# Decoder layer, attention: the turned row maxima, from a two-byte block to an f32 block

## The chip, the cores and the metric

One core of a Trainium2 chip runs the kernel. The metric is the device time of one execution in microseconds; the kernel before took 1079.38 us in the median of three runs (1075.42 to 1080.08).

## The reference

A decoder layer on x of shape (4, 512, 512) f32: attention, a quantised cross part and a feed-forward layer with routed tokens, each added to x behind a layer norm. Only attention matters here:

```
result, ch_bias, n = _chunk_decompose(hidden_states.reshape(bsz * tgt, H))
Q = (proj(q_weight, WQ, q_bias) * scaling).reshape(bsz, tgt, HEADS, HEAD_DIM)
K = proj(k_weight, WK, k_bias).reshape(bsz, tgt, HEADS, HEAD_DIM)
attn = jnp.einsum('bqhd,bkhd->bhqk', Q, K)
probs = jax.nn.softmax(attn, axis=-1)
ctx = jnp.einsum('bhqk,bkhd->bqhd', probs, V).reshape(bsz * tgt, H)
```

There are 32 heads of 16 channels, and the softmax subtracts the maximum over the keys of each row.

## The kernel before, in words

Attention runs in 32 iterations i, one for each batch and group of four heads (512 queries by 512 keys for each head). The first four and the last four are unrolled, 24 lie in a loop whose body holds four (`steps`, L351). Q and K of a group are kept as f16 parts, high and low, in rings of four buffers (QP, KP): rows 0 to 47 for two heads, rows 64 to 111 for the other two, so that two matmuls run beside each other in two halves of the array's rows.

Scores are computed twice. The first time (`scores`, L1284) queries lie on partitions: a pair of 128x512 blocks goes to two PSUM banks, and VectorE takes the negated maximum of each row (`maxima`, L854) into NM, a block of 128 queries by 16 (two halves `a` by eight steps `x`) for each iteration. This runs ahead: during iteration i, the pairs 1 to 7 are those of i+2 and pair 0 is the last one of i+1. The second time (L1332) keys lie on partitions, and two further rows of QP (rows 48, 49 and 112, 113, MROW) carry the maximum of each query as an f16 high and low part, so that the matmul subtracts it. ScalarE then takes the exponential (L1610) out of one of three PSUM banks (4, 5, 7, used in turn), and the probabilities go into f32 matmuls with V (`context`, L1315), four heads beside each other in groups of 32 columns. When all of them are done, ScalarE copies the sums out (L1601), and SP stores them.

The maxima have to come from a column per block into rows. After the last reduction of i+1, VectorE writes the high halves (L861) and the low halves (L863) into MS, 128x32 f16. TensorE turns MS at step 2 of iteration i (`turn_maxima_of`, L1292) into bank 4; this block has a place of its own in the order of the three banks (TURN = 6, behind transposed score block 5). VectorE copies the turned block to MT (L873), behind the third reduction of the iteration (TURN_STEP = 2), and SP stores MT into the two further rows of QP (`send_maxima`, L461), one DMA for each half `a`.

Every engine works through its own instructions in order, and semaphores join them. Those around the change: TensorE's turning waits for ms_ready (both small VectorE instructions) and for the exponential that frees bank 4; the copy waits for mt_ready; transposed score block 8 is the next to use bank 4, and `st_bank_free` (L1300) makes it wait for mt_copied; blocks 7 and 11 wait for the exponentials of blocks 5 and 8. SP works in the order: load of q and k for i+3 (L429), maxima of i+1 (L461), context of i-1 (L471, L472). Step 0 of the next iteration waits for the stored maxima (mrow_in). Before the first iteration there is a prologue in which the pairs of iterations 0 and 1 are computed, and the first maxima are turned.

Of the kernel before, what the change touches and what calls it, by code (L numbers as in the profile page):

```python
# [5 lines left out]
F32, BF16, F16, U32 = mybir.dt.float32, mybir.dt.bfloat16, mybir.dt.float16, mybir.dt.uint32  # L6
ALU, ACT, AX = mybir.AluOpType, mybir.ActivationFunctionType, mybir.AxisListType
RMAX = bass.bass_isa.ReduceOp.max

P = 128  # L10
# [26 lines left out]
RING = 4  # L37
MROW = 48
Q_PARTS = (0, 0, 1)
K_PARTS = (0, 1, 0)  # L40
LOW = 64
ROW_UNIT = 2.0 ** 12
# [18 lines left out]
def decoder_kernel(nc, x, fside, ctxw, wq, wk, wv, wo, wt, brows, router, w1, b1, w2, b2, out):  # L61
    ctx = ExitStack()
    with ctx:
# [3 lines left out]
        def sem(name):  # L67
            return ctx.enter_context(nc.semaphore(name))
# [10 lines left out]
        slab = [sb(f"slab{i}", [P, 8192]) for i in range(5)]  # L79
# [20 lines left out]
        CBPO = slab[4][:, 4096:4352].bitcast(BF16)  # L100
        QP = slab[2][:, 4096:6144].bitcast(F16).rearrange("p (r h q) -> p r h q", r=RING, h=2)
        KP = slab[2][:, 6144:8192].bitcast(F16).rearrange("p (r h q) -> p r h q", r=RING, h=2)
        identh = slab[2][:, 0:64].bitcast(F16)
        PROB = slab[3][:, :].rearrange("p (k h q) -> p k h q", k=KB, h=GH)
        CTX = slab[1][:, :].rearrange("p (g q) -> p g q", q=S)

# [74 lines left out]
        SWV, SWO = sb("SWV", [P, D]), sb("SWO", [P, D])  # L181
        identf, ones = sb("identf", [P, P]), sb("ones", [P, P])
# [18 lines left out]
        CBY = HB[:, 0:3]  # L201

        NM = SWV[:, 144:144 + 16 * RING].rearrange("p (r n) -> p r n", r=RING)
        MS = SWV[:, 128:144].bitcast(F16)
        MS_PARTS = MS.rearrange("p (a c n) -> p c a n", a=2, c=2)
        MT = SWV[0:32, 0:128].bitcast(F16).rearrange("p (a q) -> p a q", a=2)

        rnd = sb("rnd", [P, 4])
        below = rnd[:, 2:4]
# [55 lines left out]
        PS = ctx.enter_context(nc.psum_tensor("PS", [P, 8, 512], F32))  # L265
# [29 lines left out]
        def quantised(lo, hi):  # L295
# [16 lines left out]
        cbt_ready, dg_ready, swrow_ready, cb_ready, cbp_ready, ab_ready = (  # L312
            sem(n) for n in ("cbt_ready", "dg_ready", "swrow_ready", "cb_ready", "cbp_ready", "ab_ready"))
        qk_mm, qk_scaled, qk_h, qk_l = (sem(n) for n in ("qk_mm", "qk_scaled", "qk_h", "qk_l"))
        bound_ready, bounds_ready, scale_ready, kp_ready, identh_ready = (
            sem(n) for n in ("bound_ready", "bounds_ready", "scale_ready", "kp_ready", "identh_ready"))
        split_out = [sem(f"split_out{r}") for r in range(3)]
        v_mm, v_scaled = sem("v_mm"), sem("v_scaled")
        qk_in = [sem(f"qk_in{r}") for r in range(RING)]
        s_ready, s_free, ms_ready, mt_ready, mt_copied = (  # L320
            sem(n) for n in ("s_ready", "s_free", "ms_ready", "mt_ready", "mt_copied"))
        mrow_in = [sem("mrow_in0"), sem("mrow_in1")]
        st_ready, probs, vst_ready, pv_done, cx_copied = (
            sem(n) for n in ("st_ready", "probs", "vst_ready", "pv_done", "cx_copied"))
# [23 lines left out]
        def steps(eng, body):  # L348
            for i in range(RING):
                body(i, i)  # L350
            with eng.Fori(1, NI // RING - 1) as n:  # L351
                for r in range(RING):
                    body(n * RING + r, r)
            for i in range(NI - RING, NI):
                body(i, i % RING)
# [8 lines left out]
        TURN_STEP, TURN = 2, 6  # L364
        SBANKS = (0, 2)
        STBANK = (4, 5, 7)
# [17 lines left out]
        def exists(j):  # L384
            return not isinstance(j, int) or 0 <= j < NI
# [8 lines left out]
        def wait(eng, semaphore, value):  # L394

            if not isinstance(value, int) or value > 0:
                eng.wait_ge(semaphore, value)
# [4 lines left out]
        def _(sp):  # L402
# [54 lines left out]
            def send_maxima(j, r):  # L457

                wait(sp, mt_copied, j + 1)
                for a in range(2):  # L460
                    sp.dma_start(QP[LOW * a + MROW:LOW * a + MROW + 2, r % RING].rearrange("c h (t q) -> c (h t) q", t=4),  # L461
                                 MT[16 * a:16 * a + 16, r % 2]).then_inc(mrow_in[r % 2], 16)

            def send_context(i, r):

# [182 lines left out]
        def _(dve):  # L648
# [195 lines left out]
                    rest(u - 1)  # L844
            rest(NT - 1)
            dve.wait_ge(v_scaled, NT)
            nc.vector.tensor_copy(identh, identf[:, :]).then_inc(identh_ready, 1)

            def maxima(i, r):

                for j, ahead, x, n in pairs(i):
                    ring, bank = (r + ahead) % RING, SBANKS[x % 2]
                    dve.wait_ge(s_ready, 8 * j + x + 1)
                    nc.vector.tensor_reduce(NM[:, ring].rearrange("p (a x) -> p a x", a=2)[:, :, x], PS[:, bank:bank + 2, :], AX.X,  # L854
                                            ALU.max, negate=True).then_inc(s_free, 1)
                    if x == 7:
                        dve.wait_ge(s_free, 8 * j + 8)
                        nm = NM[:, ring].rearrange("p (a x) -> p a x", a=2)

                        wait(dve, mt_ready, j)  # L860
                        nc.vector.tensor_scalar(MS_PARTS[:, 0], nm, 1.0 / ROW_UNIT, None, ALU.mult).then_inc(ms_ready, 1)  # L861
                        dve.wait_ge(ms_ready, 2 * j + 1)
                        nc.vector.scalar_tensor_tensor(MS_PARTS[:, 1], nm, 1.0 / ROW_UNIT, MS_PARTS[:, 0], ALU.mult,  # L863
                                                       ALU.subtract).then_inc(ms_ready, 1)
                    if n == TURN_STEP and exists(i + 1):
                        turned_maxima(i + 1, (r + 1) % RING)
                if isinstance(i, int) and i == NI - 2:
                    turned_maxima(i + 1, (r + 1) % RING)

            def turned_maxima(j, ring):  # L870
                dve.wait_ge(mt_ready, j + 1)
                wait(dve, mrow_in[ring % 2], 16 * (j - ring % 2))
                nc.vector.tensor_copy(MT[:, ring % 2], PS[0:32, STBANK[TURN % 3], 0:64].bitcast(F16)).then_inc(mt_copied, 1)  # L873

            maxima(-2, -2)
            maxima(-1, -1)
# [298 lines left out]
        def _(pe):  # L1175
# [109 lines left out]
                                               start=True, stop=True)  # L1285
                    ins.then_inc(s_ready, 1)

            def turn_maxima_of(j, i):

                pe.wait_ge(ms_ready, 2 * j + 2)  # L1290
                wait(pe, probs, 16 * i + TURN - 2)
                nc.tensor.transpose(PS[0:32, STBANK[TURN % 3], 0:64].bitcast(F16), MS, identh).then_inc(mt_ready, 1)  # L1292

            def st_bank_free(i, t):
                n = st_turn(t) - 3
# [24 lines left out]
            def body(i, r):  # L1320
                if isinstance(i, int) and i == NI - 1:

                    pe.wait_ge(s_free, 8 * NI)
                for s, (k, p) in enumerate(ORDER):
                    if s == 0:

                        pe.wait_ge(mrow_in[r % 2], 16 * (i - r % 2) + 32)
                    scores(i, r, s, s + 1)
                    for a in range(2):
                        st_bank_free(i, 2 * s + a)  # L1330
                        rows = slice(LOW * a, LOW * a + MROW + 2)
                        nc.tensor.matmul(PS[:, st_bank(2 * s + a), :], KP[rows, r, p, P * k:P * k + P], QP[rows, r, p, :],  # L1332
                                         start=True, stop=True).then_inc(st_ready, 1)
                    if s < 4 and not (isinstance(i, int) and i == 0):
                        context(i - 1, (r - 1) % RING, 2 + s // 2, s % 2)
                    for k_now, half in {5: ((0, 0),), 6: ((0, 1), (1, 0)), 7: ((1, 1),)}.get(s, ()):
                        context(i, r, k_now, half)
                    if s == TURN_STEP and exists(i + 1):
                        turn_maxima_of(i + 1, i)
                    if isinstance(i, int) and i == NI - 1 and s in SPREADS:  # L1340
                        n = sum(SPREADS[q] for q in SPREADS if q < s)
                        spread(n, n + SPREADS[s])
# [15 lines left out]

            scores(-2, -2, 0, 8)
            scores(-1, -1, 0, TURN_STEP + 1)  # L1360
            pe.wait_ge(identh_ready, 1)
            turn_maxima_of(0, -1)
            scores(-1, -1, TURN_STEP + 1, 8)
            steps(pe, body)
            for k in (2, 3):
# [152 lines left out]
        def _(act):  # L1518
# [75 lines left out]
            for r in range(3):  # L1594
                act.wait_ge(split_out[r], 48 * len(range(r, NT, 3)))

            def copy_context(i, r):
                act.wait_ge(pv_done, KB * i + KB)

                wait(act, cx_out[r % 2], 40 * (i - r % 2))  # L1600
                nc.scalar.activation(CXS[:, r % 2], PS[:, 6, :], ACT.Copy).then_inc(cx_copied, 1)  # L1601

            def body(i, r):
                for t in range(16):
                    (k, p), a = ORDER[t // 2], t % 2
                    act.wait_ge(st_ready, 16 * i + t + 1)
                    if p == a == 0:

                        wait(act, pv_done, KB * (i - 1) + k + 1)
                    nc.scalar.activation(PROB[:, k, 2 * a + p], PS[:, st_bank(t), :], ACT.Exp,  # L1610
                                         scale=score_scale).then_inc(probs, 1)
                    if t == 8 and not (isinstance(i, int) and i == 0):
                        copy_context(i - 1, (r - 1) % RING)

            steps(act, body)
            copy_context(NI - 1, RING - 1)
            act.wait_ge(swi_ready, 4)
# [122 lines left out]
```

## Time and profile before

| what | value |
|---|---|
| median of three runs | 1079.38 us (1075.42 to 1080.08) |
| the profiled execution | 1075.34 us, span 1073.6 us |
| TensorE matmul busy | 795.4 us, 74% of the span |
| VectorE busy | 811.7 us, 76% |
| ScalarE busy | 603.9 us, 56% |
| row maxima (L854) | 256 instructions, mean 1218 ns |
| exponentials (L1610) | 512 instructions, mean 600 ns |

The span is the time from the first to the last instruction of the profiled execution; its own time is 1.7 us longer. A busy share says how much of the time an engine worked, and not whether anything waited for it. Times of instructions are starts and lengths in us from the start of the span. Instructions of one engine overlap by some tenths of a microsecond, so that one can start before the one ahead of it has ended.

### The profile page before, as it was taken

How to read it: one execution, taken by the hardware profiler on the slowest of the kernel's cores; microseconds unless marked ns; L12 is line 12 of the kernel's file. 1: busy time of each engine (PE TensorE's matmuls, PEld its weight loads, DVE VectorE, ACT ScalarE, POOL GpSimd, SP SyncE). 2: the span in 40 equal slices, each digit the busy share in tenths (PEclk: the TensorE clock that was granted, in tenths of full speed). 3: DMA queues.
4: the chain of work that ended last, by engine and by line, in shares of the span. 5: the costliest groups of instructions: out<-in, count | busy, mean ns of one | idle time of the engine just before them, and what ended most of it. 6: DMA issues, size and time to landing. Idle time of an engine off the chain costs nothing.

```text
span 1073.6 us, 15424 instructions
## 1 busy us (share of the span) xinstructions
PE 795.4 (74%) x5161; PEld 340.3 (32%) x5175; DVE 811.7 (76%) x1119; ACT 603.9 (56%) x1023; POOL 94.1 (9%) x212
## 2 busy tenths in 40 slices
PE   1448896999999999999734535555556268999997
PEld 1412231222222222222211123343334244444443
DVE  7899999899999999997699998688766683322111
ACT  4837332788888888888318037765563763654000
POOL 1210000000000000001000000100001252000101
PEclk9868995999999999999966857667666687999999
DMA  8400582111111112111210001100025402000000
GB/s 299 172 0 1 173 282 75 49 50 48 56 55 47 57 45 58 44 57 25 73 58 0 1 0 40 59 20 0 12 88 226 158 12 68 1 1 1 30 20 30
DMA packets 48325, 66.75 MB, mean 62 GB/s; under 512 B 11532, under 2 KB 25868, under 8 KB 47768
## 3 DMA queue, kind: packets, MB, share of 16 engines
q1 hardware_dynamic: 46488, 61.95, 17.6%
q0 software_dynamic: 1792, 4.22, 1.2%
q8 instruction: 26, 0.43, 0.2%
q14 instruction: 19, 0.16, 0.0%
HBM read 42.52 MB, written 19.19 MB: 57 GB/s over the span
## 4 chain that ended last, share of the span: by engine, by line
PE 50%; DVE 25%; ACT 11%; issue 10%; POOL 2%; DMA 1%; ACTq 1%; POOLq 0%; SPq 0%; DVEq 0%
PE PS L1315 12%; PE PS L1503 8%; PE PS L1513 8%; PE PS L1332 7%; PE PS L1284 5%; PE PS L1445 2%; PE PS L1251 2%; ACT slab L1610 2%; DVE SWV L854 2%; ACT HB L1601 2%; DVE mn L689 1%; DVE slab L782 1%; DVE slab L781 1%; PE PS L1263 1%; PE PS L1205 1%
## 5 line engine op out<-in xcount | busy, mean ns | idle before, releaser
L854 DVE TENSOR_REDUCE SWV<-PS 128x2 f32<-128x1024 f32 x256 | 303.3, 1218 | 22.3 <-PE PS L1284 18.9
L1610 ACT ACTIVATE slab<-PS 128x512 f32<-128x512 f32 x512 | 273.4, 600 | 77.9 <-PE PS L1332 71.8
L1315 PE MATMUL PS<-slab,HB 128*32 128x256 f32 x2048 | 157.6, 392 | 5.9 <-ACT HB L1601 5.9
L1332 PE MATMUL PS<-slab 50*128 50x512 f16 x512 | 139.6, 388 | 12.8 <-ACT slab L1610 10.5
L1284 PE MATMUL PS<-slab 48*128 48x512 f16 x512 | 104.0, 403 | 11.3 <-DVE SWV L854 10.2
L1503 PE MATMUL PS<-slab 128*128 128x512 f16 x384 | 86.7, 390 | 1.4 <-DVE slab L1151 1.4
L1513 PE MATMUL PS<-slab 128*128 128x512 f16 x384 | 83.0, 379 | 0.0
L1315 PEld LDWEIGHTS PS<-slab,HB 128*32 128x32 f32 x2048 | 45.0, 108 | 77.2 <-issue 70.2
L1166 DVE SCALAR_TENSOR_TENSOR slab<-HB,cmax,slab 128x512 f16<-128x512 f32 x32 | 24.0, 751 | 53.8 <-ACT slab L1706 53.8
L1332 PEld LDWEIGHTS PS<-slab 50*128 50x128 f16 x512 | 39.0, 94 | 72.7 <-ACT slab L1610 66.7
L1284 PEld LDWEIGHTS PS<-slab 48*128 48x128 f16 x512 | 24.7, 93 | 109.0 <-issue 84.5
L1170 DVE SCALAR_TENSOR_TENSOR WOT<-PS,cmax,WOT 128x512 f32<-128x512 f32 x8 | 6.0, 750 | 69.8 <-PE PS L1513 69.8
L1503 PEld LDWEIGHTS PS<-slab 128*128 128x128 f16 x384 | 38.3, 100 | 49.3 <-issue 4.8
L580 POOL COPY HB<-slab 128x64 f32 (+1 forms) x128 | 26.0, 246 | 316.2 <-PE PS L1315 315.9
L1513 PEld LDWEIGHTS PS<-slab 128*128 128x128 f16 x384 | 37.6, 98 | 45.3
L1405 PE MATMUL PS<-identf,sc 128*128 128x128 f32 x64 | 16.6, 441 | 43.1 <-DVE inv L975 43.1
L1445 PE MATMUL PS<-slab 128*128 128x512 bf16 x89 | 31.8, 531 | 15.7 <-ACT slab L1670 15.7
L1527 ACT ACTIVATE slab<-PS 128x512 f32<-128x512 f32 (+1 forms) x40 | 21.6, 626 | 38.1 <-PE PS L1205 38.1
L1587 ACT ACTIVATE slab<-slab 128x1024 f16<-128x1024 f32 x16 | 16.9, 1057 | 43.3 <-DVE slab L837 31.0
L983 DVE SCALAR_TENSOR_TENSOR slab<-PS,sc,slab 128x512 f32<-128x512 f32 x32 | 23.5, 749 | 23.5 <-PE PS L1445 22.6
L1703 ACT ACTIVATE HB<-PS,b1col,cmax 128x512 f32<-128x512 f32 x32 | 24.8, 775 | 27.9 <-PE PS L1503 27.8
L1205 PE MATMUL PS<-identf,HB 128*128 128x128 f32 x160 | 26.0, 332 | 18.8 <-DVE HB L681 8.9
(274 smaller groups left out, 1232.4 us busy)
## 6 DMA issues: line engine op xcount, KB each, us to landing
slab<-in_L_ffn_w SPq DMA_DIRECT2D x2, 4096.0 KB, 14.7
q_split<-slab SPq DMA_DIRECT2D x24, 256.0 KB, 2.6
k_split<-slab SPq DMA_DIRECT2D x24, 256.0 KB, 2.8
slab<-q_split SPq DMA_DIRECT2D x64, 96.0 KB, 2.5
slab<-k_split SPq DMA_DIRECT2D x64, 96.0 KB, 2.5
slab<-in_x SPq DMA_DIRECT2D x4, 1024.0 KB, 12.2
slab<-HB SPq DMA_DIRECT2D x128, 32.0 KB
slab<-in_fside_BxS2xS SPq DMA_DIRECT2D x4, 1024.0 KB, 5.3
```

The lines of the kernel that those rows point to most:

```text
L580: ins = nc.gpsimd.tensor_copy(VST[:, r % 2, k, :, 0:DH], src[:, k])
L854: nc.vector.tensor_reduce(NM[:, ring].rearrange("p (a x) -> p a x", a=2)[:, :, x], PS[:, bank:bank + 2, :], AX.X, ALU.max, negate=True).th ...
L1166: nc.vector.scalar_tensor_tensor(HID[h][:, 1, j], HB[:, n % 4], fhid, HID[h][:, 0, j], ALU.mult, ALU.subtract).then_inc(hid_lo, 1)
L1205: ins = nc.tensor.transpose(PS[:, 8 - banks + t % banks, P * c:P * c + P], HB[:, t % 4, P * c:P * c + P], identf[:, :])
L1284: ins = nc.tensor.matmul(PS[:, bank + a, :], QP[rows, ring, p, P * t:P * t + P], KP[rows, ring, p, :], start=True, stop=True)
L1315: ins = nc.tensor.matmul(PS[32 * h:32 * h + 32, 6, cols], VST[:, r % 2, k, h, :], PROB[:, k, h, cols], start=k == half == 0, stop=k == KB ...
L1332: nc.tensor.matmul(PS[:, st_bank(2 * s + a), :], KP[rows, r, p, P * k:P * k + P], QP[rows, r, p, :], start=True, stop=True).then_inc(st_re ...
L1445: ins = nc.tensor.matmul(PS[:, 4 * c + (2, 3, 0, 1)[t]], LXT[c][layer(n)][:, i, P * t:P * t + P], LWT[c][layer(n)][:, i], start=i == 0, st ...
L1503: ins = nc.tensor.matmul(PS[:, n % 4], W1T[:, a, i, P * j:P * j + P], XGT[:, b, i, S * h:S * h + S], start=i == 0 and a == b == 0, stop=i ...
L1513: ins = nc.tensor.matmul(PS[:, 4 + k % 2], HID[h][:, a, j, P * t:P * t + P], W2T[:, b, j], start=j == 0 and a == b == 0, stop=j == FT - 1 ...
L1610: nc.scalar.activation(PROB[:, k, 2 * a + p], PS[:, st_bank(t), :], ACT.Exp, scale=score_scale).then_inc(probs, 1)
L1703: nc.scalar.activation(HB[:, n % 4], PS[:, n % 4], ACT.Gelu, bias=b1col[:, j:j + 1], scale=fback1).then_inc(gelu_done, 1)
```

## The change

TensorE turns NM itself, as one f32 block of 16x128, and no longer MS. The two small VectorE instructions (L861, L863), the f16 identity and MS go. The turned block is in bank 4 as f32; ScalarE reads it first, right behind the exponential of block 5, and writes the high halves in f16 (`high_maxima`); then VectorE writes the low halves as the difference of the f32 block and the high halves. This last step stands behind the fourth reduction of the iteration, where the copy stood behind the third. MT now lies on 16 partitions (half `a` and step), and each of the two DMAs stores one row kind (all high or all low halves) to two partitions that lie 64 apart.

```
-        MS = SWV[:, 128:144].bitcast(F16)
-        MT = SWV[0:32, 0:128].bitcast(F16).rearrange("p (a q) -> p a q", a=2)
+        MT = SWV[0:16, 208:464].bitcast(F16).rearrange("p (r c q) -> p r c q", r=2, c=2)
@@ SP, send_maxima
-                for a in range(2):
-                    sp.dma_start(QP[LOW * a + MROW:LOW * a + MROW + 2, r % RING].rearrange("c h (t q) -> c (h t) q", t=4),
-                                 MT[16 * a:16 * a + 16, r % 2]).then_inc(mrow_in[r % 2], 16)
+                for c in range(2):
+                    sp.dma_start(QP[MROW + c:P:LOW, r % RING].rearrange("a h (t q) -> a (h t) q", t=4),
+                                 MT[:, r % 2, c]).then_inc(mrow_in[r % 2], 16)
@@ VectorE
-            nc.vector.tensor_copy(identh, identf[:, :]).then_inc(identh_ready, 1)
-                    if x == 7:
-                        dve.wait_ge(s_free, 8 * j + 8)
-                        nm = NM[:, ring].rearrange("p (a x) -> p a x", a=2)
-                        wait(dve, mt_ready, j)
-                        nc.vector.tensor_scalar(MS_PARTS[:, 0], nm, 1.0 / ROW_UNIT, None, ALU.mult).then_inc(ms_ready, 1)
-                        dve.wait_ge(ms_ready, 2 * j + 1)
-                        nc.vector.scalar_tensor_tensor(MS_PARTS[:, 1], nm, 1.0 / ROW_UNIT, MS_PARTS[:, 0], ALU.mult,
-                                                       ALU.subtract).then_inc(ms_ready, 1)
-                    if n == TURN_STEP and exists(i + 1):
+                    if n == TURN_STEP + 1 and exists(i + 1):
                         turned_maxima(i + 1, (r + 1) % RING)
             def turned_maxima(j, ring):
-                dve.wait_ge(mt_ready, j + 1)
-                wait(dve, mrow_in[ring % 2], 16 * (j - ring % 2))
-                nc.vector.tensor_copy(MT[:, ring % 2], PS[0:32, STBANK[TURN % 3], 0:64].bitcast(F16)).then_inc(mt_copied, 1)
+                dve.wait_ge(mt_high, j + 1)
+                nc.vector.scalar_tensor_tensor(MT[:, ring % 2, 1], PS[0:16, STBANK[TURN % 3], 0:P], 1.0 / ROW_UNIT,
+                                               MT[:, ring % 2, 0], ALU.mult, ALU.subtract).then_inc(mt_copied, 1)
@@ TensorE
-                pe.wait_ge(ms_ready, 2 * j + 2)
+                pe.wait_ge(s_free, 8 * j + 8)
                 wait(pe, probs, 16 * i + TURN - 2)
-                nc.tensor.transpose(PS[0:32, STBANK[TURN % 3], 0:64].bitcast(F16), MS, identh).then_inc(mt_ready, 1)
+                nc.tensor.transpose(PS[0:16, STBANK[TURN % 3], 0:P], NM[:, ring], identf[:, :]).then_inc(mt_ready, 1)
@@ ScalarE
+            def high_maxima(j, ring):
+                act.wait_ge(mt_ready, j + 1)
+                wait(act, mrow_in[ring % 2], 16 * (j - ring % 2))
+                nc.scalar.activation(MT[:, ring % 2, 0], PS[0:16, STBANK[TURN % 3], 0:P], ACT.Copy,
+                                     scale=1.0 / ROW_UNIT).then_inc(mt_high, 1)
@@ ScalarE, body, behind the exponential of block t
+                    if t == TURN - 1 and exists(i + 1):
+                        high_maxima(i + 1, (r + 1) % RING)
@@ ScalarE, ahead of the iterations
+            high_maxima(0, 0)
```

## Rows read from the trace of the kernel before

**Rows 1.** Stretches: span, busy of TensorE, its weights, VectorE, ScalarE, GpSimd, clock, DMA
```profile
179.00:190.00 11.00, 10.79 (x55) 2.53 (x53) 9.25 (x11) 7.54 (x14) 0.00 (x0) 0.50 0.04 11
300.00:400.00 100.00, 94.10 (x910) 28.87 (x911) 92.90 (x105) 84.01 (x161) 7.73 (x40) 1.00 0.18 51
```
**Rows 2.** The chain that ended last, by line, 300 to 345 us
```profile
by line: PE PS L1315 37.3%; PE PS L1332 22.3%; PE PS L1284 19.3%; issue 8.2%; ACT slab L1610 6.0%; ACT HB L1601 5.3%; ACTq L1606 1.3%; ACTq L397 0.5%; PE PS L1292 0.4%; ACTq L351 0.3%
```
**Rows 3.** Waits, 179 to 499 us: who for whom, us in total, times, longest
```profile
DVE SWV L854 <- PE PS L1284: 18.9, 60, 1.6
...
PEld PS L1284 <- DVE SWV L854: 8.7, 33, 0.6
```
**Rows 4.** VectorE in order of time: start, length, line, operation, count, idle before
```profile
308.19 1.22 DVE L854 TENSOR_REDUCE SWV<-PS 128x2 f32<-128x1024 f32 x1
...
309.65 0.17 DVE L863 SCALAR_TENSOR_TENSOR SWV<-SWV 128x16 f16<-128x16 f32 x1
309.76 2.36 DVE L854 TENSOR_REDUCE SWV<-PS 128x2 f32<-128x1024 f32 x2
...
310.91 1.22 DVE L854 TENSOR_REDUCE SWV<-PS 128x2 f32<-128x1024 f32 x1
312.04 0.20 DVE L873 COPY SWV<-PS 32x128 f16<-32x128 f16 x1
...
316.02 1.23 DVE L854 TENSOR_REDUCE SWV<-PS 128x2 f32<-128x1024 f32 x1 [0.17 <-PE PS L1284]
317.66 1.23 DVE L854 TENSOR_REDUCE SWV<-PS 128x2 f32<-128x1024 f32 x1 [0.41 <-PE PS L1284]
```
**Rows 5.** TensorE's matmuls in order of time, in and around the same iteration
```profile
302.68 0.38 PE L1332 MATMUL PS<-slab 50*128 50x512 f16 x2
...
311.43 0.22 PE L1292 MATMUL PS<-slab,SWV 128*32 128x128 f16 x1
311.58 0.39 PE L1284 MATMUL PS<-slab 48*128 48x512 f16 x2
...
313.29 0.38 PE L1332 MATMUL PS<-slab 50*128 50x512 f16 x2
...
314.44 0.39 PE L1332 MATMUL PS<-slab 50*128 50x512 f16 x1 [0.34 <-ACT slab L1610]
...
315.59 0.39 PE L1284 MATMUL PS<-slab 48*128 48x512 f16 x2
```
**Rows 6.** ScalarE in order of time, the same iteration
```profile
311.53 0.59 ACT L1610 ACTIVATE slab<-PS 128x512 f32<-128x512 f32 x1
312.23 1.09 ACT L1610 ACTIVATE slab<-PS 128x512 f32<-128x512 f32 x2
...
313.79 0.60 ACT L1610 ACTIVATE slab<-PS 128x512 f32<-128x512 f32 x1 [0.48 <-PE PS L1332]
```
**Rows 7.** SP's issue of the maxima, TensorE's next t0; q's loads to landing
```profile
312.26 1.43 SPq L461 DMA_DIRECT2D slab<-SWV  x2
...
318.56 0.83 PE L1332 MATMUL PS<-slab 50*128 50x512 f16 x2
...
slab<-q_split SPq DMA_DIRECT2D x64, 96.0 KB, 2.5
```
**Rows 8.** Single lines: shortest, median, longest in ns, first and last start
```profile
L749 DVE SCALAR_TENSOR_TENSOR ind<-cmax,mx x8: 291/291/293, 66.9 to 555.9; 128x128 f32<-128x128 f32 x8
...
L1114 DVE SCALAR_TENSOR_TENSOR slab<-PS,cmax,slab x32: 742/743/751, 856.2 to 882.8; 128x512 f16<-128x512 f32 x32
...
L1205 PE MATMUL PS<-identf,HB x160: 272/273/477, 29.2 to 906.9; 128*128 128x128 f32 x160
...
L1552 ACT ACTIVATE slab<-slab,ind x56: 331/332/348, 75.0 to 567.0; 128x64 f32<-128x64 f32 x56
```
**Rows 9.** TensorE in order of time, an unrolled iteration (i = 29)
```profile
491.88 0.39 PE L1284 MATMUL PS<-slab 48*128 48x512 f16 x2
...
493.63 0.38 PE L1332 MATMUL PS<-slab 50*128 50x512 f16 x2
```

More of the change, by code:

```diff
@@ L102, in decoder_kernel @@
         KP = slab[2][:, 6144:8192].bitcast(F16).rearrange("p (r h q) -> p r h q", r=RING, h=2)
-        identh = slab[2][:, 0:64].bitcast(F16)
         PROB = slab[3][:, :].rearrange("p (k h q) -> p k h q", k=KB, h=GH)
@@ L203, in decoder_kernel @@
         NM = SWV[:, 144:144 + 16 * RING].rearrange("p (r n) -> p r n", r=RING)
-        MS = SWV[:, 128:144].bitcast(F16)
-        MS_PARTS = MS.rearrange("p (a c n) -> p c a n", a=2, c=2)
-        MT = SWV[0:32, 0:128].bitcast(F16).rearrange("p (a q) -> p a q", a=2)
+        MT = SWV[0:16, 208:464].bitcast(F16).rearrange("p (r c q) -> p r c q", r=2, c=2)
         rnd = sb("rnd", [P, 4])
@@ L314, in decoder_kernel @@
         qk_mm, qk_scaled, qk_h, qk_l = (sem(n) for n in ("qk_mm", "qk_scaled", "qk_h", "qk_l"))
-        bound_ready, bounds_ready, scale_ready, kp_ready, identh_ready = (
-            sem(n) for n in ("bound_ready", "bounds_ready", "scale_ready", "kp_ready", "identh_ready"))
+        bound_ready, bounds_ready, scale_ready, kp_ready = (
+            sem(n) for n in ("bound_ready", "bounds_ready", "scale_ready", "kp_ready"))
         split_out = [sem(f"split_out{r}") for r in range(3)]
@@ L319, in decoder_kernel @@
         qk_in = [sem(f"qk_in{r}") for r in range(RING)]
-        s_ready, s_free, ms_ready, mt_ready, mt_copied = (
-            sem(n) for n in ("s_ready", "s_free", "ms_ready", "mt_ready", "mt_copied"))
+        s_ready, s_free, mt_ready, mt_high, mt_copied = (
+            sem(n) for n in ("s_ready", "s_free", "mt_ready", "mt_high", "mt_copied"))
         mrow_in = [sem("mrow_in0"), sem("mrow_in1")]
@@ L1286, in scores, with turn_maxima_of @@
                     ins.then_inc(s_ready, 1)
-            def turn_maxima_of(j, i):
-                pe.wait_ge(ms_ready, 2 * j + 2)
+            def turn_maxima_of(j, i, ring):
+                pe.wait_ge(s_free, 8 * j + 8)
                 wait(pe, probs, 16 * i + TURN - 2)
-                nc.tensor.transpose(PS[0:32, STBANK[TURN % 3], 0:64].bitcast(F16), MS, identh).then_inc(mt_ready, 1)
+                nc.tensor.transpose(PS[0:16, STBANK[TURN % 3], 0:P], NM[:, ring], identf[:, :]).then_inc(mt_ready, 1)
             def st_bank_free(i, t):
@@ L1338, in body @@
                     if s == TURN_STEP and exists(i + 1):
-                        turn_maxima_of(i + 1, i)
+                        turn_maxima_of(i + 1, i, (r + 1) % RING)
                     if isinstance(i, int) and i == NI - 1 and s in SPREADS:
@@ L1360, in _ @@
             scores(-1, -1, 0, TURN_STEP + 1)
-            pe.wait_ge(identh_ready, 1)
-            turn_maxima_of(0, -1)
+            turn_maxima_of(0, -1, 0)
             scores(-1, -1, TURN_STEP + 1, 8)
```

## The prediction

> **What bounds the kernel now.** I read the stretches first, to find the stage that the change touches. Attention runs from 179 to about 525 us. In its first 11 us the granted clock is 0.50 (the 1.2 GHz level), afterwards 1.00 (2.4 GHz) [rows 1]. From 300 to 400 TensorE is busy 94.10 us, VectorE 92.90, ScalarE 84.01 [rows 1]. With three engines this full the busy shares don't name the bound, so I went to the chain. By line it consists almost wholly of TensorE's three matmul lines, with ScalarE's exponentials (L1610) and context copy (L1601); no VectorE line is in it [rows 2]. The waits agree: the row-maximum reductions (L854) waited 18.9 us for score matmuls in 60 places, while TensorE's score weights waited 8.7 us for reductions in 33 [rows 3].
>
> Then one iteration, engine by engine. I call TensorE's eight steps s0 to s7, the reduction that follows each score pair n0 to n7, and the sixteen transposed score matmuls t0 to t15 (two a step). t8 starts at 302.68 and again at 313.29: a period of 10.61 us [rows 5]. VectorE has two holes in it, 0.17 and 0.41 us, both ended by a score pair [rows 4]: it has 0.58 us to spare. TensorE is stopped by ScalarE: t11 at 314.44 waited until the exponential of t8 had freed its bank [rows 5, 6]. So the path through an iteration is TensorE, the exponential of t8, t11, the context matmuls, and on. What moves t8 moves the end; what only lightens VectorE does not.
>
> t8 takes the PSUM bank in which the turned maxima lie, so it waits for mt_copied, the end of VectorE's last work on them. Before, that is the copy at 312.04, 0.20 long [rows 4]: over at 312.24, a full 1.05 us ahead of t8. This slack is what the change spends.
>
> **The change, part by part.** All times are put on the iteration that has its t8 at 313.29.
>
> 1. *The two small VectorE instructions (L861, L863) go.* n0 starts at 308.19 and n1 at 309.76 [rows 4]. A reduction behind another starts 1.15 us after it (n1 at 309.76, n2 at 310.91), so the pair costs 1.57 - 1.15 = 0.42 us of VectorE. n1 needs its own score pair, though. A reduction starts 0.43 us after its pair (315.59 to 316.02 [rows 4, 5]), and in this trace n1 is already nearly that close to its pair, so 0.05 us is all that it gains. Worth to the path: nothing, since the path doesn't pass through VectorE.
>
> 2. *The turning becomes f32.* Now 0.22 us at 311.43, with the next score pair 0.15 behind it [rows 5]. The f32 turning of 128 columns on L1205 takes 0.272 at best against 0.22 here [rows 8]: +0.05 for the maxima to be ready, and, since I take the array to be held longer by as much, +0.05 for the pair of s3, from 311.58 to 311.63. Its wait moves from the small instructions to n0's end, both long over.
>
> 3. *ScalarE writes the high halves, behind the exponential of t5.* That exponential starts at 311.53; the next engine slot is 0.49 later (two exponentials back to back take 1.09, one 0.60 [rows 6]), at 312.02; the maxima are ready at 311.43 + 0.27 = 311.70, so ScalarE doesn't wait. The trace has no activation of 16x128. From below 0.2 us is the least that I allow; from above 0.59, the 512-column one; the nearest row is 64 columns, 0.332 [rows 6, 8]. I take 0.35 for its duration and half of that for the slot. The exponential of t6 starts at 312.23 now [rows 6], so most of the slot falls in a hole of 0.2 us. A delay of 0.15 at t6 would be hidden again before t8, where ScalarE sits idle 0.48 us [rows 6]. Cost: 0. If that cover were gone, it would be the slot, 0.2 to 0.5 us an iteration. High halves ready: 312.4.
>
> 4. *VectorE's last step moves behind one more reduction and becomes longer.* It stood behind n2, it will stand behind n3. n3 starts 0.43 behind the pair of s3: 311.63 + 0.43 = 312.06. An instruction behind a reduction starts 1.13 us after the reduction's start (310.91 to 312.04 [rows 4]): 313.19. By then the high halves have been there for 0.8 us. Its duration: the same operation on 128x128 takes 0.291 (L749, from SBUF); 128x16 takes 0.17 (L863), 128x512 out of PSUM 0.743 (L1114) [rows 4, 8]. The last two are the ends, and I take 0.29, the row with the same count of elements. It ends at 313.48. From a releasing end to the matmul that waits for it is 0.05 us (the exponential of t8, 313.79 + 0.60, to t11 at 314.44 [rows 5, 6]). **t8 starts at 313.53 and no longer at 313.29: +0.24 us.**
>
> In sentences of its own: on the copy's row, 0.20 us for 128 two-byte elements a partition, against 0.29 for the f32 operation. The Trainium skill (VectorE: DVE Perf Modes, "Why PSUM operands drop a tier") says that an operand in PSUM leaves a two-byte operation at most two elements a cycle and an f32 one a single element, which speaks against replacing a two-byte copy by an f32 operation. By that rule the step gets longer, the trace's rows agree in size; had the rate stayed, t8 would be 0.15 us late instead of 0.24.
>
> 5. *What the later t8 moves.* t9, s5, t10, the exponential of t8 and, through it, t11 and the context copy all start 0.24 later; the waits for ScalarE repeat at the same distances. On VectorE n4 follows s4 (unchanged) at 313.49 and n5 is held by n4; the holes before n6 and n7 grow. Nothing between t8 and the next s3 had been waiting for VectorE by more than 0.07 us (s5, and that falls behind t8 now), so nothing gives the 0.24 back. The new period is 10.85.
>
> 6. *The stores.* Still two DMAs of 4 KB. They are issued at 312.26 and take SP 1.43 [rows 7]; they move to 313.5 and end at 314.95. Behind them on SP wait the five context stores, which are released by the end of the context copy, behind t8's exponential: 313.79 + 0.49 + 0.59 = 314.87 before, and 0.24 more now: not delayed. Landing: the first s0 that needs the rows is t0 at 318.56 [rows 7], 3.6 us after the issue ends; the loads of q and k, over twenty times as large, land 2.5 us from their issue [rows 7]. Cost 0; if the cover were gone, its excess over 3.6. ScalarE takes over VectorE's wait for the stores of two iterations before, long landed.
>
> 7. *How many iterations.* 24 run in the loop (i = 4 to 27) at 0.24: 5.8 us. The five unrolled ones at full clock (1, 2, 3, 28, 29) have s3 at 491.88 and t8 at 493.63 [rows 9], 1.75 us apart; the new way from the old s3 to t8 is 0.05 + 0.43 + 1.13 + 0.29 + 0.05 = 1.95, so +0.20 each: 1.0 us. In i = 30 there is no n3 and the step follows the high halves at once: 0. Ahead of i = 1, at 1.2 GHz, VectorE is the bound. There the change takes 0.42 - 0.09 = 0.33 us from VectorE once in the prologue: -0.3. I count i = 0 as nothing (the same gain again, against a late t8), and so the conversion of the identity to f16 that falls away (one small instruction).
>
> Sum: 5.8 + 1.0 - 0.3 = **+6.5 us**. The profiled execution took 1075.34 us (span 1073.6 and 1.7 around it); with 6.5 it would be 1081.8. It is among the fastest that are shown: the median of the three timed runs is 1079.38. I predict for a median: 1079.4 + 6.5 = 1085.9, rounded 1086.
>
> **The rivals.**
> - *VectorE is the bound after all: faster.* It decides if the two holes of 0.58 us are only echoes of VectorE's own lateness. Then an iteration is worth 0.42 (the small pair) less 0.09 (0.29 against 0.20) = 0.33 us, times 30: -10, 1069.5. For it: 92.9% busy, 8.7 us of waits of score weights. Against: those waits end ahead of other waits, and no VectorE line is in the chain. 9%.
> - *The lateness is absorbed: no change.* The step takes 0.17 as with 16 elements and the turning costs TensorE nothing: +0.07 an iteration, 2 us, 1081. Against: the 128x128 row. 18%.
> - *ScalarE's copy lands on the path.* Place: between t5 and t6. If it holds its engine for a full 0.59 and its waits are handled one after another, t6 and t7 slip by over 0.5 and the idle 0.48 before t8 is used up; then t8's exponential comes later too, by up to 0.3 more: 30 x 0.3 = +9, 1095. Nothing in rows 6 speaks for so long a slot. 7%.
> - *The PSUM operation is as dear as the 512-column one (0.74).* +0.45 x 29 = +13 more, 1099. 3%.
> - My forecast, +4 to +11 us: 63%.
>
> **From cases to numbers.** Runs of this kernel spread by 0.4%, so 0.5% (5.4 us) is about what can be told from no change. Faster: 9%. Of the forecast's own part, a good three quarters lie above 5.4 us (its 0.24 would have to be under 0.20 to miss it): 49%, with the two dearer rivals 59%. No change: 14 + 18 = 32%. The range takes in the absorbed case below and most of the ScalarE case above, and that the profiled execution is 4 us under the median: 1079 to 1093.
>
> **What the changed profile would show.** The f32 turning at about 0.27 and s3 0.2 behind it (step 2); the 16x128 activation starting straight behind t5's exponential, and the exponential of t8 still with an idle stretch before it (3); the VectorE operation near 0.29, 1.13 behind n3's start, and t8 0.05 behind its end, named as its releaser (4); a period of 10.85 (5); stores that end before the context stores are due (6). The prediction is wrong if t8 is released by anything but that operation, if the period is not over 10.7, or if VectorE's holes close.

## The result, and the profile after

The changed kernel takes 1090.48 us in the median of four runs (1086.88 to 1091.46), the kernel before 1079.47 in its four. The ratio is 1.0104, with a 95% interval of 1.007 to 1.0138: slower, by 11 us. The profiled execution took 1091.28 us (span 1089.5).

Of the 15.9 us between the two profiled executions, 10.65 lie in attention. From the start of the first score pair to the start of the last context matmul the kernel before takes 159.87 to 524.90, that is 365.03 us, the changed one 161.69 to 537.37, 375.68 us. Another 1.8 us lie ahead of it and 3.5 behind it, where nothing was changed. Other kernels of this study start attention anywhere from 159.6 to 162.2, so I take this for a spread between executions; the medians are 11 us apart.

VectorE and TensorE are both less busy than before over the same 100 us, the granted clock is the same (against [rows 1]; columns as there):

```profile
300.00:400.00 100.00, 92.80 (x889) 28.85 (x890) 87.39 (x82) 82.46 (x166) 6.97 (x36) 1.00 0.18 49
```

VectorE is 5.5 us lighter in 100. About 3 of these are only the longer iterations (3.4% fewer of them fit in); the rest is lighter work, and it did not make the kernel faster. The chain by line (305 to 350 us), which held no VectorE line before [rows 2], now has two, the low halves (L859) and the reduction ahead of them (L850), and twice the "issue", time in which the engine on the chain waited for nothing that the profile shows:

```profile
by line: PE PS L1302 31.7%; PE PS L1319 17.7%; issue 17.4%; PE PS L1271 15.2%; ACT slab L1603 6.0%; ACT HB L1594 5.3%; DVE SWV L859 2.5%; PE PS L1279 1.9%; DVE SWV L850 1.4%; ACTq L1599 1.2%; ACTq L348 0.3%; ACTq L394 0.3%
```

The added "issue" is one piece of 0.99 us in each iteration. The chain in order of time (start, length) shows where it lies: on VectorE, between the start of the fourth reduction and the low halves, while that reduction runs (its row, 318.04 and 1.23 long, stands below):

```profile
318.04 0.15 DVE SWV L850
318.19 0.99 issue
319.18 0.28 DVE SWV L859
319.46 0.05 issue
319.50 0.48 PE PS L1319 x2
```

The waits from 179 to 499 us show the same (who for whom, total us, times, longest):

```profile
DVE SWV L850 <- PE PS L1271: 37.2, 86, 1.6
...
PEld PS L1319 <- DVE SWV L859: 15.1, 29, 1.3
...
PEld PS L1279 <- ACT slab L1603: 9.9, 24, 0.4
```

The reductions wait twice as long for score matmuls as before [rows 3]; TensorE's weights wait for the low halves 29 times, once in each iteration of this stretch. One iteration of TensorE's matmuls, to be laid beside [rows 5]:

```profile
308.51 0.47 PE L1319 MATMUL PS<-slab 50*128 50x512 f16 x2 [0.20 <-DVE SWV L859]
...
316.82 0.64 PE L1302 MATMUL PS<-slab,HB 128*32 128x256 f32 x8
317.39 0.28 PE L1279 MATMUL PS<-identf,SWV 128*16 128x128 f32 x1
317.60 0.39 PE L1271 MATMUL PS<-slab 48*128 48x512 f16 x2
317.83 0.57 PE L1319 MATMUL PS<-slab 50*128 50x512 f16 x2
318.33 0.64 PE L1302 MATMUL PS<-slab,HB 128*32 128x256 f32 x8
318.90 0.39 PE L1271 MATMUL PS<-slab 48*128 48x512 f16 x2
319.50 0.47 PE L1319 MATMUL PS<-slab 50*128 50x512 f16 x2 [0.21 <-DVE SWV L859]
...
320.66 0.39 PE L1319 MATMUL PS<-slab 50*128 50x512 f16 x1 [0.34 <-ACT slab L1603]
```

t8 starts at 308.51 and at 319.50: the period is 10.99 us, 0.37 more than 10.61 (10.987 and 10.613 in the unrounded times). It is released by the low halves, and no longer by its own place in the order. VectorE and ScalarE in the same iteration, beside [rows 4, 6]:

```profile
318.04 1.23 DVE L850 TENSOR_REDUCE SWV<-PS 128x2 f32<-128x1024 f32 x1
319.18 0.27 DVE L859 SCALAR_TENSOR_TENSOR SWV<-PS,SWV 16x128 f16<-16x128 f32 x1
319.37 2.34 DVE L850 TENSOR_REDUCE SWV<-PS 128x2 f32<-128x1024 f32 x2
```
```profile
317.37 0.59 ACT L1603 ACTIVATE slab<-PS 128x512 f32<-128x512 f32 x1
317.85 0.25 ACT L1587 ACTIVATE SWV<-PS 16x128 f16<-16x128 f32 x1
318.25 1.08 ACT L1603 ACTIVATE slab<-PS 128x512 f32<-128x512 f32 x2
320.01 0.60 ACT L1603 ACTIVATE slab<-PS 128x512 f32<-128x512 f32 x1 [0.68 <-PE PS L1319]
```

n3 at 318.04, the low halves 1.14 behind it, ending at 319.45, t8 0.05 behind that. ScalarE's high halves are done at 318.10, a full microsecond before VectorE comes to use them, and ScalarE then stands idle for 0.68 us ahead of t8's exponential. All of this is the forecast's picture. What it had not is the start of the turning. Weight loads around it, first before, then after:

```profile
311.22 0.10 PEld L1292 LDWEIGHTS PS<-slab,SWV 128*32 128x32 f16 x1
```
```profile
317.06 0.40 PE L1302 MATMUL PS<-slab,HB 128*32 128x256 f32 x4
...
317.39 0.09 PEld L1279 LDWEIGHTS PS<-identf,SWV 128*16 128x16 f32 x1 [0.41 <-ACT slab L1603]
```

A context step runs in two passes of four matmuls. Before, the second pass starts at 311.22, the turning's weights go in at the same moment, and the turning starts at 311.43, 0.21 behind (0.215 in the unrounded times). After, the second pass starts at 317.06 and the weights go in only at 317.39, together with the turning: 0.33 behind. The f32 turning starts 0.115 us later behind the context's second pass than the two-byte one, in every iteration but the first, in which no context stands ahead of it.

### The profile page after: what moved, and what is told of

The parts are those of the page before. It is cut to its first block, busy times and chain, and to the rows that moved or that the text cites. A ratio compares the mean times of both kernels' runs of the same rounds, so it can differ in the third digit from the quotient of the medians.

```text
span 1089.5 us, 15374 instructions
## 1 busy us (share of the span) xinstructions
PE 805.8 (74%) x5175; PEld 341.9 (31%) x5175; DVE 805.7 (74%) x1054; ACT 608.6 (56%) x1055; POOL 94.3 (9%) x212
## 4 chain that ended last, share of the span: by engine, by line
PE 49%; DVE 25%; issue 12%; ACT 11%; POOL 2%; DMA 1%; ACTq 0%; POOLq 0%; SPq 0%; DVEq 0%
PE PS L1302 10%; PE PS L1489 8%; PE PS L1499 8%; PE PS L1319 6%; PE PS L1271 5%; DVE SWV L850 3%; PE PS L1431 2%; PE PS L1238 2%; ACT slab L1603 2%; ACT HB L1594 2%; DVE mn L686 1%; PE PS L1250 1%; PE PS L1216 1%; PE PS L1192 1%; ACT slab L1666 1%
## 5 line engine op out<-in xcount | busy, mean ns | idle before, releaser
L850 DVE TENSOR_REDUCE SWV<-PS 128x2 f32<-128x1024 f32 x256 | 303.5, 1218 | 41.9 <-PE PS L1271 38.7
L1603 ACT ACTIVATE slab<-PS 128x512 f32<-128x512 f32 x512 | 273.3, 599 | 71.9 <-PE PS L1319 64.8
L1319 PE MATMUL PS<-slab 50*128 50x512 f16 x512 | 136.5, 389 | 18.5 <-ACT slab L1603 10.4
L1271 PE MATMUL PS<-slab 48*128 48x512 f16 x512 | 105.9, 403 | 10.8 <-DVE SWV L850 9.8
L1431 PE MATMUL PS<-slab 128*128 128x512 bf16 x96 | 34.2, 531 | 13.4 <-ACT slab L1666 13.4
```

The source lines that it names most:

```text
L1271: ins = nc.tensor.matmul(PS[:, bank + a, :], QP[rows, ring, p, P * t:P * t + P], KP[rows, ring, p, :], start=True, stop=True)
L1431: ins = nc.tensor.matmul(PS[:, 4 * c + (2, 3, 0, 1)[t]], LXT[c][layer(n)][:, i, P * t:P * t + P], LWT[c][layer(n)][:, i], start=i == 0, st ...
```

## The experiments

I had two parts to separate (the place of the last step, and the turning), and then the reason of the late turning. Lengths of attention are first score pair to last context matmul, as above; ratios are against the kernel before on the same chip.

**e1: the changed kernel with the low halves behind n2.**

```diff
-                    if n == TURN_STEP + 1 and exists(i + 1):
+                    if n == TURN_STEP and exists(i + 1):
```

> The changed kernel, but the low halves are written behind n2 again (where the copy stood), not behind n3. My theory: what lengthened the period from 10.61 to 10.99 us is the later release of t8, by one more reduction ahead of it. Then t8 is free of VectorE again, VectorE waits a little for ScalarE's high halves ahead of its step, and the period goes back to 10.61 to 10.65: about 11 us less than the changed kernel, 1079 to 1080, level with before. Rival (the f32 turning and ScalarE's step themselves cost the time on TensorE and ScalarE): the period stays above 10.85 and at most 4 us come back.

Measured: 1073.45 us, ratio 0.9991 (0.9979 to 1.0003) against 1074.19. The whole loss is gone. Attention takes 364.28 us, 0.75 less than before; the period is 10.61:

```profile
301.91 0.38 PE L1319 MATMUL PS<-slab 50*128 50x512 f16 x2
...
312.52 0.38 PE L1319 MATMUL PS<-slab 50*128 50x512 f16 x2
```

VectorE now waits 0.21 us for the high halves, in time that it has to spare:

```profile
308.95 2.36 DVE L850 TENSOR_REDUCE SWV<-PS 128x2 f32<-128x1024 f32 x2 [0.31 <-PE PS L1271]
311.52 0.28 DVE L859 SCALAR_TENSOR_TENSOR SWV<-PS,SWV 16x128 f16<-16x128 f32 x1 [0.21 <-ACT SWV L1587]
311.73 3.47 DVE L850 TENSOR_REDUCE SWV<-PS 128x2 f32<-128x1024 f32 x3
```

The low halves end at 311.80, 0.72 us ahead of t8. The f32 turning, its late start and ScalarE's step are all still in this kernel and cost nothing: t6 comes later, but t7, which waits for the exponential of t5, starts 0.96 us behind the context's second pass as before. So they cost something only when VectorE's last step stands behind the fourth reduction.

**e2: the turned block 32 columns wide.** Sixteen unused columns are turned with the maxima.

```diff
-        NM = SWV[:, 144:144 + 16 * RING].rearrange("p (r n) -> p r n", r=RING)
+        NMW = SWV[:, 0:32 * RING].rearrange("p (r n) -> p r n", r=RING)
+        NM = NMW[:, :, 0:16]
-                nc.tensor.transpose(PS[0:16, STBANK[TURN % 3], 0:P], NM[:, ring], identf[:, :]).then_inc(mt_ready, 1)
+                nc.tensor.transpose(PS[0:32, STBANK[TURN % 3], 0:P], NMW[:, ring], identf[:, :]).then_inc(mt_ready, 1)
```

> The changed kernel, but NM has 32 columns an iteration (16 used) and the f32 turning takes all 32. In the changed kernel the turning starts 0.33 us behind the start of the context's last pass, before it started 0.21 behind; its weights are loaded only after the matmuls. Theory geometry (a block of 16 columns is not of the width of the context's 32-column blocks, so its weights can't go in while those run): the turning is 0.21 behind again, t8 comes 0.12 earlier, period 10.87, some 3.4 us less than the changed kernel. Theory type (f32 maxima as weights) or theory wait (it waits for the reductions' semaphore now): still 0.33, period 10.99.

Measured: 1085.49, ratio 1.0118 (1.0093 to 1.0143), period 10.99, attention 375.67 against 375.68. The theory of the block's width is refuted. The second pass of the context starts 0.24 behind 314.67, at 314.91, and the weights again come 0.33 behind it, at 315.24:

```profile
314.67 0.16 PEld L1303 LDWEIGHTS PS<-slab,HB 128*32 128x32 f32 x8 [0.23 <-issue]
315.24 0.09 PEld L1280 LDWEIGHTS PS<-identf,SWV 128*32 128x32 f32 x1 [0.41 <-ACT slab L1604]
```

**e3: e1 and e2 together.** Edits as above.

> Both: low halves behind n2, and 32 columns turned. Theory: the period is that of before, 10.61, and the prologue is 0.3 to 0.5 us shorter, so 1079, level with before; the 0.12 of the turning is hidden ahead of t7, which waits for the exponential of t5, and so makes no difference to e1_order. Rival (the turning is on the path of its own): e3 is 3 us faster than e1.

Measured: 1074.57, ratio 1.0001 (0.9986 to 1.0016), period 10.61. No difference to e1 that could be told. As e2 had not moved the turning, this says no more than e1. The shorter prologue that was expected can't be read from the length of attention, 365.53 us in this trace: the granted clock fell to 0.93 from 499 to 525 us, where the other traces have 1.00.

**e4: the kernel before with its copy behind n3.**

```diff
-                    if n == TURN_STEP and exists(i + 1):
+                    if n == TURN_STEP + 1 and exists(i + 1):
```

> The kernel before with one edit: its copy stands behind n3, not n2; all else is old (two small VectorE instructions, two-byte turning, two-byte copy). By the sum of the prediction t8 is then released at s3 + 0.43 + 1.13 + 0.20 + 0.05, that is 1.82 behind s3 against 1.71 now: +0.11 us an iteration in the loop, 0.06 unrolled, together +3 us: 1082.5. Rival (the position costs nothing, the kinds of instruction do): 1079.5.

Measured: 1080.03, ratio 1.0058 (1.0041 to 1.0074) against 1074.19, +5.8 us where I had expected 3; attention takes 369.49 us, 4.46 more than before. The position alone makes t8 wait for VectorE:

```profile
314.81 0.20 DVE L873 COPY SWV<-PS 32x128 f16<-32x128 f16 x1
```
```profile
313.08 0.22 PE L1292 MATMUL PS<-slab,SWV 128*32 128x128 f16 x1
313.23 0.39 PE L1284 MATMUL PS<-slab 48*128 48x512 f16 x2
...
315.07 0.47 PE L1332 MATMUL PS<-slab 50*128 50x512 f16 x2
```

t8 is at 315.07, 1.84 behind s3, where it was 1.71 [rows 5]. The period is 10.76, so the position costs 0.15 us an iteration (I had expected 0.11; n3 starts 0.45 behind its pair and not 0.43, and t8 is 0.06 behind the copy's end and not 0.05). The other 0.22 of the change's 0.37 only count because the position has put VectorE's step in front of t8. Set side by side, the traces of e4 and of the changed kernel differ by the late start of the turning (0.115), its longer hold of the array (0.06) and the longer last step (0.07), less 0.02 because n3 again starts 0.43 behind its pair: together 0.22.

**e5: the turning as an ordinary matmul.**

```diff
-                nc.tensor.transpose(PS[0:16, STBANK[TURN % 3], 0:P], NM[:, ring], identf[:, :]).then_inc(mt_ready, 1)
+                nc.tensor.matmul(PS[0:16, STBANK[TURN % 3], 0:P], NM[:, ring], identf[:, :],
+                                 start=True, stop=True).then_inc(mt_ready, 1)
```

> The changed kernel, with the turning as an ordinary f32 matmul against the identity and not as a transpose. e2 has ruled out the width of the block: the turning still starts 0.33 us behind the start of the context's last pass (0.215 before). Theory mode (the array has to change from f32 matmul to f32 transpose, and so the weights can't be loaded under the context's matmuls): as a matmul it is 0.215 behind, like the second pass of the context itself; it takes two passes of 0.107, so s3 comes about 0.05 earlier or at the same time as in the changed kernel, period 10.94 to 10.99. Theory wait or theory block (no 128x16 f32 weights load under a matmul): 0.33 again, s3 0.1 later, period 11.1, some 3 us over the changed kernel.

Measured: 1083.76, ratio 1.0093 (1.0057 to 1.013), period 10.98. Weight loads and matmuls around the turning:

```profile
316.29 0.31 PEld L1279 LDWEIGHTS PS<-identf,SWV 128*16 128x16 f32 x2
```
```profile
316.51 0.38 PE L1279 MATMUL PS<-identf,SWV 128*16 128x128 f32 x2
316.82 0.39 PE L1271 MATMUL PS<-slab 48*128 48x512 f16 x2
```

The second pass of the context starts at 316.29 here, the turning's weights go in at 316.29 beside it, and the matmul starts 0.215 behind. Same data, same width, same f32, same two waits: only the transpose is gone, and with it the delay. The f32 product takes two passes (x2), s3 starts 0.31 behind the turning and no longer 0.21, and that takes the gain back.

**e6: the wait for the reductions ahead of the context.**

```diff
+                    if s == TURN_STEP and exists(i + 1):
+                        pe.wait_ge(s_free, 8 * (i + 1) + 8)
                     if s < 4 and not (isinstance(i, int) and i == 0):
                         context(i - 1, (r - 1) % RING, 2 + s // 2, s % 2)
@@ turn_maxima_of
-                pe.wait_ge(s_free, 8 * j + 8)
@@ ahead of the first turning
+            pe.wait_ge(s_free, 8)
```

> The changed kernel, with TensorE's wait for the reductions (s_free) ahead of the context matmuls of step 2, not between them and the turning. Theory wait (a semaphore that is waited for in between holds the weights back): the turning is 0.215 behind the context's last pass and the period 10.87. Theory mode: 0.33 again, 10.99.

One run, 1088.3 us, so only its trace is used. Period 10.99, the weights 0.33 behind the second pass again (context from 317.31, turning at 317.88, 0.57 apart as 316.82 and 317.39 in the changed kernel):

```profile
317.31 0.64 PE L1301 MATMUL PS<-slab,HB 128*32 128x256 f32 x8
317.88 0.28 PE L1278 MATMUL PS<-identf,SWV 128*16 128x128 f32 x1
```

So it isn't that wait. Nor is it the other one, which the profile names ("<-ACT slab L1603"): the exponential of t3 that frees the bank starts at 316.35 and takes 0.59, so it ended at 316.94, ahead of the second pass at 317.06. The name is only that of the last semaphore; and e5 has both waits too and no delay. What is shown: the f32 transpose, behind the context's f32 matmuls, starts 0.115 later than an f32 matmul or a two-byte transpose at the same place. Why the array does this stays open, and so does whether it would behind other matmuls.

**e7: e1, and one of ScalarE's waits a place earlier.** In the loop the exponential of t8 starts 0.50 us behind the start of its matmul (313.29 to 313.79 [rows 5, 6]), in unrolled iterations 0.41. Two waits stand ahead of it in both, for its matmul and for the context (pv_done). In the loop, where the values waited for come from registers, the chain of the kernel before has a register operation (ACTq L397) between the end of the matmul and the exponential; e8's, which lacks the second wait here, has the exponential at once:

```profile
313.45 0.26 PE PS L1332 x2
313.71 0.02 ACTq L397
313.74 0.05 issue
313.79 0.05 ACT slab L1610
```
```profile
313.04 0.26 PE PS L1332 x2
313.30 0.03 ACT slab L1612
```

The edit puts that wait ahead of the exponential of t7; it also drops the one ahead of t12, where the exponential starts 0.41 behind its matmul with it and without it.


```diff
-                    if p == a == 0:
+                    if p == a == 0 and k < 2:
                         wait(act, pv_done, KB * (i - 1) + k + 1)
+                    if t == 7:
+                        wait(act, pv_done, KB * (i - 1) + 3)
```

> e1_order with one edit on ScalarE: its wait for the context of two steps before (pv_done) stands ahead of the exponential of t7 and not of t8, and the one at t12, which the context copy's own wait covers, goes. In the loop the exponential of t8 starts 0.50 us behind its matmul, unrolled 0.41. Theory (the second wait with a register value ahead of the exponential of t8 costs these 0.085 us, on the path): the loop's period goes from 10.61 to 10.53, 24 x 0.085 = 2 us less than e1_order, ratio 0.997 to before. Rival (only the place of the cost moves): no change.

Measured: 1070.98, ratio 0.997 (0.9951 to 0.9988) against 1075.89: 0.3% under before, and the fastest of all. t8 is at 303.44 and 313.96, a period of 10.53 with the rounding; its exponential starts 0.42 behind it:

```profile
303.44 0.38 PE L1319 MATMUL PS<-slab 50*128 50x512 f16 x2
...
313.96 0.38 PE L1319 MATMUL PS<-slab 50*128 50x512 f16 x2
```
```profile
314.38 0.60 ACT L1605 ACTIVATE slab<-PS 128x512 f32<-128x512 f32 x1 [0.22 <-PE PS L1319]
```

**e8: the same wait in the kernel before.** Edit as in e7, on the kernel before.

> The kernel before with e7's edit on ScalarE's waits and nothing of the change. Theory (the gain of e7_order_waits is that of the wait, not of the turned f32 block): the loop's period is 10.53 here too and the ratio to before 0.998, 24 x 0.085 = 2 us faster. Rival (only with the lighter VectorE does the earlier exponential of t8 pay): the period stays at 10.61.

Measured: 1079.19 against 1080.65, ratio 0.9986 (0.9967 to 1.0005), which by itself can't be told from no change. In the trace the period is 10.53 and attention takes 362.99 us, 2.0 less than before. e7's takes 362.28. So e7's gain is that of the wait, for 2.0 us (e1 to e7: 364.28 to 362.28 too). Some 0.7 us are left for the lighter VectorE, 0.52 of them ahead of the first t0, at the slow clock.

## Why the prediction was right, and where it was short

The direction, the mechanism and the place were right: 1086 was forecast with 1079 to 1093, and 1090.5 came. The added time was forecast at 6.5 us and was 11. That 1090.5 still lies in the range owes something to luck: the room above was there for ScalarE's copy on the path, and what filled it was mostly a late turning, which no rival had. Point by point:

1. *The small pair is worth nothing on the path.* Shown by e1, which lacks it and has the old period. VectorE's relief shows only where VectorE was the bound: from the first score pair to t0 of the first iteration the kernel before takes 159.87 to 179.16, the changed one 161.69 to 180.45, 0.52 us less. I had 0.3.
2. *The f32 turning: this term was too small.* I priced it at +0.05 for s3, by the longer hold of the array. That came as +0.06 (s3 is 0.21 behind the turning and no longer 0.15). But I let it start where the two-byte turning started, and it starts 0.115 later, because its weights don't go in beside the context's matmuls. So s3 came 0.17 later than before, against 0.05. This is the missing term: 24 x 0.115 = 2.8 us in the loop and 0.6 unrolled. e2 rules out the width, e6 the wait for the reductions, and e5 shows that it is the transpose: the same f32 block as a matmul starts on time.
3. *ScalarE's step costs nothing.* Right: 0.25 long (I took 0.35). The exponential of t6 starts 0.40 behind it, at 318.25, but that is 0.42 behind its own matmul (317.83), as before (311.81 to 312.23), so it was not held up. The idle stretch before t8's exponential grew from 0.48 to 0.68. The rival of ScalarE's copy on the path is refuted, and so is that of the dear PSUM operation.
4. *VectorE's last step.* 0.27 long for 0.29, 1.14 behind n3 for 1.13, t8 0.05 behind its end. From the turning's start to t8 it is 2.11 us in the trace; by my terms it is 0.05 + 0.15 + 0.43 + 1.13 + 0.29 + 0.05 = 2.10. The position and its effect are shown from both sides by e1 and e4. On the Trainium skill's rule (VectorE: DVE Perf Modes, "Why PSUM operands drop a tier"): the trace agrees in direction, 0.27 for the f32 operation against 0.20 for the two-byte copy; the two differ in kind and in partitions as well, so no run here isolates the rule.
5. *Nothing gives it back.* Right: the distance from t8 to t11 is 1.16 (319.50 to 320.66), and was 1.15.
6. *The stores are hidden.* Right: they are issued at 319.47 in 1.22 us, and the first context store follows at 321.23, when its own wait ends.
7. *The count.* 24 x 0.374 = 9.0 in the loop and 5 x 0.33 = 1.6 unrolled, 0.5 gained in the prologue. I had set the first iteration to nothing; from its turning to the next it takes 13.41 us after and 12.72 before, so it lost 0.7. Some of that belongs to the clock and not to the change: the mean granted clock of this stretch was 0.65 against 0.67 before, and e2, with 0.67, took 13.20. Sum 10.8, for 10.65 measured in attention.

The rival of the bound on VectorE is refuted by e1, whose VectorE is lighter at the old period, that of the absorbed lateness by the period.

## What to carry to other kernels

An instruction on an engine that isn't the bound has slack only up to the wait that hangs on it: here 1.05 us, and one reduction of 1.15 placed ahead of it spent it all. Before a step is moved behind one more instruction, look up who waits for its semaphore and lay that wait's time beside the new end. Once such a wait is on the path, what is added upstream is paid in each iteration (here 0.22 us for a later and longer turning and a longer last step), while in the old order it cost nothing.

## What the runs showed that I had not expected

- The f32 transpose behind the context's f32 matmuls started 0.33 us after their last pass began; a two-byte transpose and an f32 matmul of the same block 0.215. Its weights were not loaded beside the running matmuls.
- A second wait ahead of the exponential of t8, on a value in a register, cost 0.085 us an iteration in the loop (10.61 to 10.53 in e7 and e8), though it had long been satisfied. In the kernel before, the exponentials of t0 and t2, which have a second wait too, also start 0.50 us or more behind their matmul in the loop and 0.41 in unrolled iterations; that of t12 starts at 0.41 in both, so it is not a rule for every second wait. In unrolled iterations, whose waits are on constants, the period was 10.53 from the start.
